# Attention on one core: value products A1 and A2 share a PSUM bank with the small unit in front of them

## The reference

```python
x = x + tanh(g_xattn[0]) * xattn(layernorm(x), ctx_1024, mask, Wq, bq, Wk, bk, Wv, bv, Wo, bo)
x = x + tanh(g_ffn[0])   * ffn(layernorm(x), w1, b1, w2, b2, w3, b3, gate_w, gate_b)

# xattn, 16 heads of 32
q, k, v = h @ Wq.T + bq, ctx @ Wk.T + bk, ctx @ Wv.T + bv
scores = einsum('bhnd,bhtd->bhnt', q, k) / sqrt(32) + mask
out = einsum('bhnt,bhtd->bhnd', softmax(scores), v) @ Wo.T + bo
# ffn: softmax router over 8 experts, the top 2 of each row,
# each expert gelu(gelu(x w1 + b1) w2 + b2) w3 + b3, weighed with its gate and summed
```

## Time and profile before

| | |
|---|---|
| median of 3 runs | 1812.67 us (1810.89 to 1813.68) |
| the profiled execution | 1812.63 us, of it a span of 1810.7 us |
| TensorE busy | 1769.7 us, 98% of the span |
| VectorE busy | 1171.3 us, 65% |
| ScalarE busy | 962.8 us, 53% |
| granted TensorE clock, mean | 0.994 |

### The profile page before, as it was taken

How to read it: one execution, slowest core, us unless ns; L and a number is a source line. 1 busy time by engine, 2 the same in 40 slices (tenths; PEclk the granted TensorE clock), 3 DMA queues, 4 the chain that set the end, 5 groups by cost and what they waited for, 6 DMA issues and landing times.

```text
span 1810.7 us, 39486 instructions
## 1 busy us (share of the span) xinstructions
PE 1769.7 (98%) x14832; PEld 1534.9 (85%) x14832; DVE 1171.3 (65%) x3158; ACT 962.8 (53%) x1794; POOL 120.9 (7%) x159
## 2 busy tenths in 40 slices
PE   7999999999999999999998999999999999999997
PEld 7788888888888888888887778778799999999996
DVE  4566667666666676676666456565677777777772
ACT  3566555655565565556555534454555555555551
POOL 1110000000000000000000001000000110100110
PEclk9999999999999999999999899999999999999998
DMA  7892112112211211121004259999766666666661
GB/s 228 307 341 72 38 53 62 39 31 59 59 42 31 59 44 32 52 63 38 27 26 146 93 204 393 369 349 307 236 216 215 215 215 215 215 214 210 210 200 36
DMA packets 114268, 269.72 MB, mean 149 GB/s; under 512 B 15284, under 2 KB 33716, under 8 KB 114129
## 3 DMA queue, kind: packets, MB, share of 16 engines
q1 hardware_dynamic: 99664, 225.46, 37.4%
q0 software_dynamic: 14464, 42.35, 7.8%
HBM read 221.10 MB, written 46.66 MB: 148 GB/s over the span
## 4 chain that ended last, share of the span: by engine, by line
PE 92%; DVE 3%; DMA 2%; ACT 2%; issue 1%; POOL 0%; DVEq 0%; ACTq 0%; SPq 0%; POOLq 0%
PE bank_rows L2147 21%; PE bank_rows L657 15%; PE bank_rows L643 15%; PE bank_rows L705 8%; PE bank_rows L2162 6%; PE bank_rows L716 4%; PE bank_rows L2201 4%; PE bank_rows L695 4%; PE bank_rows L2228 3%; PE bank_rows L2187 3%; PE bank_rows L680 3%; PE bank_rows L732 2%; PE bank_rows L795 2%; DMA stage<-in_L_ffn_w 1%; DVE k_low L1333 1%; ACT k_high L1039 1%
## 5 line engine op out<-in xcount | busy, mean ns | idle before, releaser
L1063 ACT ACTIVATE probs<-probs,neg_max 100x722 f32<-100x722 f32 x248 | 220.7, 891 | 99.6 <-DVE neg_max L1367 99.6
L1360 DVE CUSTOM_DVE_ANT_0 probs<-bank_rows,mask_sb 100x362 f32<-100x362 f32 x496 | 234.8, 530 | 18.8 <-PE bank_rows L695 8.7
L2391 DVE TENSOR_TENSOR w_low<-stage,w_high 128x1024 fp32r<-128x1024 f32 x176 | 213.2, 1223 | 36.6 <-ACT w_high L2295 35.8
L1068 ACT ACTIVATE p_t<-bank_rows 121x600 f32<-121x600 f32 x256 | 172.0, 672 | 73.0 <-PE bank_rows L705 69.0
L2295 ACT ACTIVATE w_high<-stage 128x1024 fp32r<-128x1024 f32 x176 | 184.0, 1058 | 35.2 <-DMA stage<-in_L_ffn_w 34.8
L2147 PE MATMUL bank_rows<-h_low,w_high 128*128 128x256 f32 x704 | 199.2, 283 | 0.0
L2147 PE MATMUL bank_rows<-h_high,w_low 128*128 128x256 f32 x704 | 199.2, 283 | 0.0
L2147 PE MATMUL bank_rows<-h_high,w_high 128*128 128x256 f32 x704 | 199.2, 283 | 0.0
L2318 ACT ACTIVATE gelu<-bank_rows,biases 128x256 f32<-128x256 f32 x176 | 82.4, 475 | 218.4 <-PE bank_rows L2147 212.7
L643 PE MATMUL bank_rows<-ctx_high,wk_high 128*128 128x360 f32 (+1 forms) x512 | 183.5, 358 | 8.8 <-DVE ctx_low L1326 8.1
L705 PEld LDWEIGHTS bank_rows<-ident,probs 100*121 100x121 f32 x1488 | 161.4, 156 | 30.6 <-ACT probs L1063 9.1
(11 more groups left out here) (244 smaller groups left out, 3732.2 us busy)
## 6 DMA issues: line engine op xcount, KB each, us to landing
stage<-in_L_ffn_w SPq DMA_DIRECT2D x240, 512.0 KB, 4.7
plain_w<-in_L_ffn_w SPq DMA_DIRECT2D x15, 2048.0 KB, 12.1
expert_in_rows<-filling POOLq DMA_DIRECT2D x8, 3341.0 KB, 16.1
ctx_raw<-in_ctx SPq DMA_DIRECT2D x16, 720.0 KB, 4.4
ctx_raw<-in_ctx SPq DMA_DIRECT2D x15, 724.0 KB, 5.0
xs_sb<-expert_in_rows SPq DMA_DIRECT2D x11, 514.0 KB, 5.2
b_sb<-in_L_ffn_b SPq DMA_DIRECT2D x19, 256.0 KB, 4.9
mask_sb<-in_mask_BxSxS_ff SPq DMA_DIRECT2D x16, 282.0 KB
```

Of the source, the lines that this page charges most:

```text
L1063: nc.scalar.activation(p, p, ACT.Exp, bias=neg_max[:, h:h + 1], scale=-1.0, accum_out=exp_sum[:, h:h + 1]).then_inc(probs_ready, 1)
L1068: nc.scalar.activation(p_t[:, h % HQ, :, :].rearrange("t (k i) s -> t k (i s)", k=2), bank_rows[0:TT, 4:6, 0:3 * S], ACT.Copy).then_inc(pt ...
L1360: nc.vector.tensor_tensor_reduce(out=probs_of(b, g)[:, q, at], in0=score_bank[q][0:S, 0:size], in1=mask_sb[:, at], scale=-1.0, scalar=BIG, ...
L2391: nc.vector.tensor_tensor(lo, src, hi.bitcast(F32), ALU.subtract).then_inc(chunk_lo[which], 1)
```

## The change

Two things change. First, the pairs (LG, A1) and (CNT, A2): when A1 stands right behind LG, or A2 right behind CNT, it takes the same bank as that small unit, and the alternation goes on from there. This is done twice in a body, so that the units outside of A1 to CNT keep their banks. Second, VectorE's queue: `logits_out` and `place` stand ahead of `keys_low` of K20 and K30 and no longer behind it, and the row maximum and the subtraction are now a function of their own, `logits_less_max`, which in bodies 1 to 14 comes after `scale_o` of A1. In the last body it stays directly behind `logits_out`. The work itself is the same, instruction for instruction.

```diff
--- before.py
+++ after.py
@@ -210,20 +210,27 @@
 LAST_QUERIES = tuple("Q" if u == "Q01" else u for u in EVEN_BODY if u != "XT")
 LAST_BODY = ("A3", "Y", "A0", "X2T", "A1", "LG", "A2", "CNT")
 PRO = -1
+SAME_BANK = {("LG", "A1"), ("CNT", "A2")}
 
 
 ALL_UNITS = {}
 FILLS = [0, 0]
+_next = 0
 for body in range(PRO, B + 1):
-    for _i, name in enumerate({PRO: PROLOGUE, 0: FIRST_BODY, B - 2: LAST_QUERIES, B - 1: LAST_BODY, B: AFTER_LAST
-                               }.get(body, ODD_BODY if body % 2 else EVEN_BODY)):
-        _bank = 0 if body == B - 1 else _i % 2 if body == B else sum(FILLS) % 2
+    _names = {PRO: PROLOGUE, 0: FIRST_BODY, B - 2: LAST_QUERIES, B - 1: LAST_BODY, B: AFTER_LAST
+              }.get(body, ODD_BODY if body % 2 else EVEN_BODY)
+    for _i, name in enumerate(_names):
+        if _i > 0 and (_names[_i - 1], name) in SAME_BANK:
+            _next = 1 - _next
+        _bank = 0 if body == B - 1 else _i % 2 if body == B else _next
+        _next = 1 - _next
         FILLS[_bank] += 1
         ALL_UNITS[body, name] = _bank, FILLS[_bank]
 SECOND_BANK_FILLS = ALL_UNITS[B, "A3"][1] - 1
 
 
 def unit(body, name):
+
 
 
     return ALL_UNITS[body, name]
@@ -1415,9 +1422,11 @@
 
         def logits_out(body, t):
             bank, done = take(body, "LG")
-            _, fills = unit(body, "LG")
             nc.vector.tensor_tensor(logits[:], bank[0:S, 0:E], gb_sb[:], ALU.add).then_inc(done, 1)
-            dve.wait_ge(done, fills)
+
+        def logits_less_max(body, t):
+            bank, fills = unit(body, "LG")
+            dve.wait_ge(emptied[bank], fills)
             route_then(t, 1, nc.vector.reduce_max(row_max[:], logits[:], AX.X))
             route_then(t, 2, nc.vector.tensor_scalar(shifted[:], logits[:], row_max[:, 0:1], None, ALU.subtract))
 
@@ -1610,13 +1619,15 @@
             recips(b, 1)
 
             score(b, 2, 0)
-            keys_low(b, n, 2, 0)
             if t is not None:
                 logits_out(b, t)
-            else:
+            keys_low(b, n, 2, 0)
+            if t is None:
                 norm_in(2)
             score(b, 2, 1)
             scale_o(b, b, 1)
+            if t is not None:
+                logits_less_max(b, t)
             values_out(b, 1 - odd, 4 if t is not None else 5)
             if b + 2 < B:
                 ln_apply(0, b + 2, x_ln[:], xn[:], xn_ready)
@@ -1631,9 +1642,9 @@
             recips(b, 2)
 
             score(b, 3, 0)
-            keys_low(b, n, 3, 0)
             if t is not None:
                 place(b, t)
+            keys_low(b, n, 3, 0)
             score(b, 3, 1)
             scale_o(b, b, 2)
             if after is not None:
@@ -1695,6 +1707,7 @@
             residual_add(b + 1, b)
             norm_out(b)
             logits_out(b + 1, b)
+            logits_less_max(b + 1, b)
             choose(b)
             carry(b)
             place(b + 1, b)
```

## The result

| | before | changed |
|---|---|---|
| median, first measurement | 1812.63 us (1810.89 to 1815.88, 6 runs) | 1801.13 us (1799.59 to 1802.89, 6 runs) |
| median, second measurement | 1811.8 us (20 runs) | 1801.9 us (5 runs) |
| ratio, first and second | | 0.9941 [0.993, 0.9952] and 0.9941 [0.9927, 0.9954] |
| profiled execution, span | 1812.63, 1810.7 us | 1801.66, 1799.7 us |

The change makes the kernel faster. The ratio of 0.9941 is 10.7 us of 1812, by its first interval 8.7 to 12.7 us; forecast were 9.5 us and a time of 1803.2 us.

The account below looks back on a forecast made before the run. The prediction took TensorE to bound the kernel, busy 1769.7 of 1810.7 us. Removing waits at A1 and A2, 14 x (0.19 + 0.49) = 9.5 us, gave 1812.67 - 9.5 = 1803.2 us, range 1799.8 to 1807.0.

Parts of the forecast that it names:

- 14 x 0.68 = 9.5 us: Bodies 1 to 14: each was to lose its waits at A1 and A2, 0.19 + 0.49 us, 9.5 us together.
- the two terms: Late starts behind k_low in each of bodies 1 to 14: 0.19 us at A1 and 0.49 us at A2.
- the fourteen waits at A1: Bodies 1 to 14: waits for k_low said to hold only the weight load; 29 weight-load waits against 15 matmul waits.
- A2's margin: CNT's bank was to be free at 406.64, 0.13 us before A2's unheld start; 0.07 us with the slower pick-up.
- Rival 1: CNT's two small instructions release A2 late; 1804.5 to 1807 us, chance 0.12.
- 0.1 us closer to their transposes: Behind A2 TensorE gains 0.49 us, VectorE only 0.4; costed at nothing, without cover 1.4 us.
- The cover of 2.5 us for the router's exponential: shifted ready at 394.8, ScalarE's exponential starting at 397.47; over 2.5 us of cover for the later maximum.
- Rival 2: Last body's cold clock stretches fall otherwise, 1.7 to 3.4 us either way; chance 0.17, half on each side.
- Rival 3: Another wait holds TensorE instead, for instance transposes waiting for p_t copies; 1812.7 to 1809.1 us, chance 0.06.
- Rival 4: Late shifted stops ScalarE's queue at the router's exponential; 1817.2 us if 3.5 us later, chance 0.03.

Follow-up runs that it names:

- A2 only: Changed kernel with VectorE's queue and the bank of group 2 (LG, A1) as before, only (CNT, A2) changed; 1805.51 us, ratio 0.9965.
- A1 only: Changed kernel with VectorE's queue and the bank of group 3 (CNT, A2) as before, only (LG, A1) changed; 1808.44 us, ratio 0.9981.
- one more step: Changed kernel plus one small VectorE instruction in bodies 1 to 14, behind the wait for CNT and ahead of row_of; 1801.54 us, ratio 0.9942.
- order only: Changed kernel's VectorE queue, but every unit in the bank it had before (SAME_BANK empty); 1810.62 us, ratio 0.9994.
- maximum ahead: Changed kernel with logits_less_max directly behind logits_out, ahead of keys_low of K20; 1802.34 us, ratio 0.995.
- banks only: Changed kernel's banks, but VectorE's queue as before, k_low ahead of logits or place; 1816.35 us, ratio 1.0024.
- its second run: The changed kernel measured and profiled again without an edit, beside the kernel before on the same chip; 1801.9 us, ratio 0.9941.
- maximum late: Changed kernel with logits_less_max moved further back, behind V4 and the layernorm of batch b+2; 1810.17 us, ratio 0.9989.
- the one with three: Changed kernel plus three small VectorE instructions (0.57 us) in bodies 1 to 14, behind the wait for CNT; 1807.79 us, ratio 0.9977.

## Why the prediction was right

**The sum.** 14 x 0.68 = 9.5 us was right to the hundredths where it can be read by itself: held 2.60 + 6.85 = 9.45 us before, 0 after. A2 only and A1 only show the two terms apart. The measured median, 1801.13, lies 2.1 us below the forecast of 1803.2. Of these 0.6 us are the rest, below; the other 1.5 us are less than the interval of the ratio allows either way, and the second measurement, 9.9 us between its medians, does not have them.

**A reading that was wrong.** The prediction says that the fourteen waits at A1 hold only the weight load back, and not the array. The array did stand idle there. In body 5 the last scores end at 391.59 + 0.33 = 391.92 and A1 starts at 392.04, and in a window around it TensorE was busy for 1.18 of 1.30 us:

```profile
391.59 0.33 PE L695 MATMUL bank_rows<-k_high,q_low 32*100 32x360 f32 x4
391.00:392.30 1.30, 1.18 (x27) 0.84 (x30) 0.84 (x4) 0.28 (x1) 0.00 (x0) 1.00 0.00 0
```

The trace has 0.11 to 0.12 us of idle time before A1 in each of bodies 1 to 14. The rows of waits don't list a wait this short, which is why they count 15 and not 29. The sum did not suffer, as it was taken from start to start: 0.12 us idle and the 0.07 us behind the modelled end are the 0.19 us.

**The margins.** A2's margin was worked out as 0.13 us, with a pick-up of CNT of 0.04 us. The trace shows both numbers, and one more step of 0.2 us, which held A2 for 0.06 us, gives the margin from the other side. Rival 1 (A2 released late) did not happen in the changed kernel; the kernel with one more step is what it would look like, and it is cheap.

**The moves on VectorE.** score(2,1) was forecast 0.65 us earlier and score(3,1) 0.4 us. Counted from the first matmul of their scores on TensorE, score(2,1) started 392.73 - 391.18 = 1.55 us behind the scores' first matmul before and 388.67 - 387.72 = 0.95 after, 0.60 earlier; score(3,1) 407.69 - 406.10 = 1.59 and 403.49 - 402.44 = 1.05, 0.54 earlier. That is more than A2's 0.49, so the exponentials did not come 0.1 us closer to their transposes, as the prediction had allowed for. That the earlier scores give TensorE nothing is shown by order only, which has them without a gain, and by maximum ahead, whose score(2,1) comes later than the changed kernel's without a hold. The cover of 2.5 us for the router's exponential was 393.81 (its start, below) - 391.28 (end of shifted) = 2.5:

```profile
393.81 0.20 ACT L1086 ACTIVATE gates<-shifted 100x8 f32<-100x8 f32 x1
```

**What the sum left out.** The rest, 0.6 us. In before, VectorE started two k_low late, in bodies 4 and 7; body 4:

```profile
339.27 0.56 ACT L1039 ACTIVATE k_high<-bank_rows,bk_sb 128x360 fp32r<-128x360 f32 x1 [0.40 <-PE bank_rows L643]
...
340.32 0.59 DVE L1333 SCALAR_TENSOR_TENSOR k_low<-bank_rows,bk_sb,k_high 128x360 fp32r<-128x360 f32 x1 [1.73 <-ACT k_high L1039]
340.97 0.43 PE L643 MATMUL bank_rows<-ctx_high,wk_high 128*128 128x362 f32 x1 [0.17 <-DVE k_low L1333]
```

k_high ended at 339.83, and k_low started 0.49 us later, 0.35 more than it takes elsewhere (0.14 for the same tile in body 6); K30, which needs that tile's bank, waited. By the start times of both traces TensorE lost 0.24 us there and as much in body 7. The same two late starts are in A2 only, banks only and maximum ahead, at the same instructions; in the changed kernel, its second run, A1 only, order only and maximum late they are gone, and one stands in body 3 where nobody waits for it (k_low at 288.53). The rest of the table follows them: 840.0 to 840.4 where the maximum stands ahead of score(2,1), 839.4 to 839.5 where it is behind scale_o. So 0.5 to 0.6 us of the gain came with moving the maximum, and by luck.

It is luck because what counts is the place of an instruction in VectorE's queue, not what the instruction does. Count VectorE's instructions in a trace from 0, those that only wait included. Before, the two late k_low are numbers 831 and 1343, which is 6 x 128 + 63 and 10 x 128 + 63. In the changed kernel the late one is number 703, 5 x 128 + 63. In all eleven traces each late k_low of bodies 1 to 14 is number 63 of a group of 128, though most such places show no late start. The kernels with the maximum ahead of score(2,1) have 4010 instructions of VectorE in the trace. The changed kernel, its second run, A1 only, order only and maximum late have 4024, one more wait in each of 14 bodies, and that moves every later instruction to another number (the page's count of all instructions shows it too: 39486 before, 39500 after). The kernel with one more step has 4038 and no late k_low in bodies 1 to 14; the one with three has 4066 and one, number 1599 = 12 x 128 + 63, at 605.56, where TensorE lost nothing. Behind each of them, 0.7 to 1.9 us later, a packet of 8192 bytes starts on queue 14, which the page lists as one that loads instructions (before: 341.2 and 528.3; changed: 290.4). So the late starts go with the loading of VectorE's instructions; that the loading causes them is not shown, as no run changed it alone.

**The clock.** Rival 2 gave 1.7 to 3.4 us either way. The profiled executions of before and after had the same clock (0.88 in the last body; 0.73, 0.88 and 0.94 in the three stretches of the earlier trace rows moved by 10.55 us, against 0.73, 0.89 and 0.93), so the difference between these two owes it next to nothing; but the runs vary by it. Over the eleven profiles the last body took 57.3 to 57.5 us at a mean of 0.88, 55.5 to 56.6 at 0.91, 54.8 at 0.94, up to 2.8 us for the same work. The Trainium skill, page "TensorE: Matmul & The Clock Gate", Part 1 on the HAM clock gate, says that one kernel shows a different number of matmuls at the lower clock from run to run, counted at its start. The two runs of the changed kernel agree that it varies, though in their last body (57.27 us at 0.88 and 54.80 us at 0.94). So rival 2 was real in its size and did not decide the result.

**The other rivals.** Rival 3 (the gain goes elsewhere): the waits of TensorE show no new row, and A1 only and A2 only add up. Rival 4 (slower by the router's exponential): the cover of 2.5 us was there, and it takes a move past V4 and the layernorm to use it up.

**What is left open.** The two medians differ by 11.5 us in the first measurement and 9.9 in the second. Holds and rest are 10.1 us; what lies between is within the intervals and can't be settled by them.

## What to carry to other kernels

Where buffers alternate by count, ask for each unit who empties the other buffer, how many engines that takes in turn, and whether the unit in between is free sooner; then change both, the buffer and the reader's place in its queue, since here the place alone gave nothing and the bank alone cost 4 us. Measure short waits by comparing start to start with a twin that doesn't wait: A1's 0.19 us stood in no row of the matmuls' waits, only in that of the weight loads, and was a quarter of the gain. Work out the margin of the new release beside its gain; with 0.13 us of it, one more step of 0.2 us in front of it is nearly free, and three cost 6 us. And when a change only moves instructions, count them: a difference of half a microsecond can come from the numbers that the later ones get.

## What the runs showed of the hardware

VectorE has late starts of about 0.35 us at fixed places of its queue, in these eleven traces number 63 of a group of 128 instructions, each followed by a packet on the queue that loads instructions. They stood at the same instructions in both profiles of the changed kernel and in all four kernels with 4010 instructions of VectorE, and moved where the count changed (bodies 4 and 7, or body 3). In the last body the granted clock differs from run to run of the same program, and with it 2.5 us of time, about a quarter of the gain that was measured here. That is why the holds had to be read from the traces, where they repeat to 0.04 us over 14 bodies.
